# Transformer stack on one core: the feed-forward norm's bias moves ahead of a copy on ScalarE

## The chip, the cores and the metric

The kernel runs on one NeuronCore of a Trainium2 chip, in one launch. The metric is the device time of the whole program in microseconds (us), lower is better. The engines are named as in the profile: PE is TensorE (PEld its weight loads), ACT is ScalarE, DVE is VectorE, POOL is GpSimd, SP issues DMAs. Each engine takes its instructions strictly in the order in which they are written, and waits on semaphores.

## The reference, cut to what matters

The input is `x` of shape (2, 1024, 128) in float32. Four residual blocks follow each other, each behind a layer norm: a causal attention with 16 heads, a stack of six layers, a gated recurrent attention, and the same stack again. The change is in the stack. One of its layers computes:

```python
def ffn_layer(x, g, bln, W1, b1, W2, b2):
    mu = x.mean(-1, keepdims=True)
    var = ((x - mu) ** 2).mean(-1, keepdims=True)
    xn = (x - mu) / jnp.sqrt(var + 1e-05) * g + bln
    hg = xn @ W1 + b1
    a, gate = jnp.split(hg, 2, -1)
    return a * jax.nn.gelu(gate, approximate=False) @ W2 + b2
for i in range(DEPTH):                                   # DEPTH = 6
    x = attn_layer(shift_tokens(x), Wqkv[i], q_scale[i], k_scale[i], Wo[i]) + x
    x = ffn_layer(shift_tokens(x), ln_g[i], ln_b[i], W1[i], b1[i], W2[i], b2[i]) + x
```

`attn_layer` is attention over a local window with 16 heads of 64: it projects q, k and v, normalises q and k, rotates them, takes a softmax over a band of keys, multiplies by v and projects back. The term `+ bln` is the one that moves.

## The kernel before, in words

Activations are kept transposed, 128 features on the partitions and 2048 tokens along the free axis, in four chunks of 512 tokens. A stack is one block of instructions for each engine, a software pipeline over *slots*. A slot takes up a new unit of attention work (a pair of heads on one chunk, 32 units in a layer) and works on older units in their later stages: in the code `a` is the unit begun in this slot, `b` the one begun two slots earlier, `d` four slots earlier. A layer has 32 slots; the layers run in a loop (`pipelined`), with the first and the last partly written out. No scheduler decides the order: each engine does what its function `slot(j, unit)` writes, top to bottom, and semaphores tie the engines together.

The feed-forward part of the same or the previous layer is threaded into these slots. A chunk needs six *steps*, 0 to 5, in six successive slots: mean (0), variance (1), three tiles of hidden features (2, 3, 4: for each, one product for `a` and one for the gate), and the gelu (5). `step` is the step that the slot begins, `before` the one of the slot before. Two chunks are done in each half layer. Step 2 always falls in a slot with odd `j`, as step 4 does, and in odd slots ScalarE also has the inverse norms of q and k (three instructions, lines 1080 to 1085). The last two chunks of each stack are done after the loop by other code, so step 2 occurs 2 stacks x (24 - 2) = 44 times.

What stands around the change in a step-2 slot, by engine:

- DVE multiplies the centred values by the gain and the inverse deviation (line 1268, semaphore `f_norm`).
- ACT does the inverse norms, copies the attention output `oT` out of PSUM (line 1119, `o_cp`), copies the projected values `va` out of PSUM bank 0 (line 1125, `va_cp`), adds the norm's bias in place on `fin` (line 1132, `f_in`; `fin` shows as tile `cen` in the profile), and then takes the eight exponentials of the softmax (line 1138, `exp_done`).
- PE projects the values (line 982, `va_mm`), multiplies `oT` by `wo` (line 996, after `o_cp`), makes the first hidden products from `fin` (line 1003 after `f_in`, line 1018), and opens the next slot with the q product into bank 0 (line 930, after `va_cp`), then lines 939 and 942.
- In the next slot DVE makes the split (line 1235), the copy of the first hidden tile (line 1243) and the product of line 1257; ACT copies the gate (line 1092), which line 949 on PE waits for; POOL adds the halves of the rotation (line 841) once SP's swapping DMAs have landed.

In a chunk that is the first of its layer, line 1003 also waits for the feed-forward weights (`ffw_ld`).

Of the kernel before, what the change touches and what calls it, by code (L numbers as in the profile page):

```python
# [9 lines left out]
ACT = mybir.ActivationFunctionType  # L10
# [40 lines left out]
ONE = 1  # L51
# [575 lines left out]
def stack(rep, ln_call, S, nc, w, c, bank, wide, xT, y, ident, identb, jmean, ln_eps, ss_eps, ss_back,  # L627
# [3 lines left out]
    with ExitStack() as st:  # L631
        def sb(name, shape, dt=F32):
            return st.enter_context(nc.sbuf_tensor(f"b{rep}_{name}", shape, dt))
# [11 lines left out]
        lng = sb("lng", [P, 2])  # L645
# [21 lines left out]
        fin, gel = cen[:, 0, :], cen[:, 1:1 + FT, :]  # L667
# [14 lines left out]
        def twos(u):  # L682
            return PER // 2 * (L0 + u[0]) + u[1] // 2
# [16 lines left out]
        def ffn(u):  # L700
            if u is None or ending(u) or u[1] % HALF >= 2 * FSTEPS:
                return None, None, None
            which, step = divmod(u[1] % HALF, FSTEPS)
            k = 2 * (u[1] // HALF) + which
            return step, k, NC * (L0 + u[0]) + k
# [22 lines left out]
        with nc.Block() as block:  # L728
# [334 lines left out]
            def _(act):  # L1063
# [3 lines left out]
                def slot(j, unit, act=act):  # L1067
                    a, b, d, f, f0 = unit(0), unit(2), unit(4), unit(FLAG), unit(FLAG + 1)
                    step, fk, C = ffn(f)
# [7 lines left out]
                    def inverse_norms(n):  # L1077
                        act.wait_ge(S["ss_mm"], ONE + n + 1)
                        act.wait_ge(S["split_done"], ONE + n)
                        act.activation(rn[:, :], bank[2][:, :], ACT.Ln, bias=ss_eps[:, 0:1], scale=SS_SCALE)\  # L1080
                            .then_inc(S["ln_done"], 1)
                        act.wait_ge(S["ln_done"], ONE + n + 1)
                        act.activation(rhi[:, :], rn[:, :], ACT.Exp, bias=ss_back[:, 0:1], scale=-0.5).then_inc(S["hi_done"], 1)
                        act.wait_ge(S["hi_done"], ONE + n + 1)
                        act.activation(rn[:, :], rn[:, :], ACT.Exp, bias=ss_back[:, 0:1], scale=-0.5).then_inc(S["rn_done"], 1)
# [31 lines left out]
                    if d:  # L1117
                        act.wait_ge(S["pv_mm"], ONE + 2 * UD + 2)
                        act.activation(oT[:, kd % 2, :], bank[7], ACT.Copy).then_inc(S["o_cp"], 1)  # L1119
                    if before == 5:  # L1120
                        act.preload_act_table_set("natural_log_exp_and_others")
                    if a:
# [4 lines left out]
                            .then_inc(S["va_cp"], 1)  # L1127
                    if a and j % 2 and before == 5:
                        inverse_norms(twos(a))
                    if step == 2:  # L1130
                        act.wait_ge(S["f_norm"], ONE + C + 1)
                        act.activation(fin, fin, ACT.Identity, bias=lng[:, 1:2]).then_inc(S["f_in"], 1)
                    if b:
                        UB, kb = um(b)
                        act.wait_ge(S["smax_done"], ONE + UB + 1)
# [5 lines left out]
                    if step == 5:  # L1141
                        act.preload_act_table_set("gelu_and_others")
                        act.wait_ge(S["f_gcp"], ONE + FT * C + FT)
                        act.activation(gel, gel, ACT.Gelu).then_inc(S["f_gelu"], 1)
                pipelined(act, PER, DEPTH, LAG, slot)

                def last_shift(n, act=act):
# [967 lines left out]
```

## Time and profile before

| what | value |
|---|---|
| time, median of 3 runs | 4369.92 us (4368.14 to 4377.39) |
| the profiled execution | 4373.69 us, its span 4372.0 us |
| PE busy | 4078.6 us, 93% |
| DVE busy | 3362.0 us, 77% |
| ACT busy | 3109.2 us, 71% |
| POOL busy | 1797.4 us, 41% |
| mean share of the 16 DMA engines that one queue (q1) takes | 36.7% |

Busy time is summed over the whole span, which the two stacks make up for the most part. Matmuls are pipelined and their ends are modelled, so where PE loses time it shows best as the distance between the starts of two instructions, compared with the same two elsewhere.

### The profile page before, as it was taken

To read this page: it belongs to the slowest core of one execution; us is meant where nothing else is said; L and a number is where in the kernel's file an instruction comes from. 1 tells how busy PE (TensorE), PEld (TensorE's weight loads), DVE (VectorE), ACT (ScalarE), POOL (GpSimd) and SP (SyncE) were. 2 spreads that over 40 slices of the span, in tenths; PEclk is the share of its full clock that TensorE was granted. 3 is DMA by queue.
4 is the path that set the end of the run, shared out by engine and by line. 5 is a ranking of instruction groups with operands and counts; after the bars stand their busy time and mean duration, and the time that the engine had idled before them with its cause. 6 is when DMAs were issued, how large, how long until landed. Compare 5 with 4: busy or idle time off the path is not lost. (4 is left out here: it accounts for less than half of the span.)

```text
span 4372.0 us, 111762 instructions
## 1 busy us (share of the span) xinstructions
PE 4078.6 (93%) x43089; PEld 2415.8 (55%) x43089; DVE 3362.0 (77%) x4981; ACT 3109.2 (71%) x7032; POOL 1797.4 (41%) x1071
## 2 busy tenths in 40 slices
PE   7997999999999999999967589999999999999998
PEld 3443555555555555555536545555555555555554
DVE  5774888888888888888735478888888888888885
ACT  3555777777777777777762267777777777777776
POOL 3112444444444444444404534444444444444442
PEclk7997999999999999999986599999999999999999
DMA  2212444444443444444300044444444444444342
GB/s 43 31 21 72 96 110 101 106 95 103 104 104 93 112 103 96 106 98 104 80 10 3 3 111 107 103 94 106 108 96 109 99 105 96 103 103 107 93 100 49
DMA packets 232516, 380.70 MB, mean 87 GB/s; under 512 B 59365, under 2 KB 122337, under 8 KB 231689
## 3 DMA queue, kind: packets, MB, share of 16 engines
q1 hardware_dynamic: 231560, 372.20, 36.7%
q8 instruction: 370, 6.06, 0.6%
q10 hardware_dynamic: 384, 0.79, 0.1%
q14 instruction: 202, 1.65, 0.1%
HBM read 39.22 MB, written 1.05 MB: 9 GB/s over the span
## 5 line engine op out<-in xcount | busy, mean ns | idle before, releaser
L835 POOL TENSOR_TENSOR b_prob<-b_prob,b_rinv 128x768 f32<-128x768 f32 x384 | 564.2, 1469 | 1797.0 <-DVE b_rinv L1276 1797.0
L841 POOL TENSOR_TENSOR b_prc<-b_prc,b_sws 128x1024 f32<-128x1024 f32 x384 | 906.7, 2361 | 70.8 <-DMA b_sws<-b_prs 70.6
L1138 ACT ACTIVATE b_prob<-ps,b_nmx 128x96 f32<-128x96 f32 x3072 | 748.9, 362 | 0.0
L1211 DVE SCALAR_TENSOR_TENSOR b_prc<-ps,b_qks,b_rot 128x512 f32<-128x512 f32 x768 | 570.6, 743 | 11.8 <-ACT b_sq L1099 11.5
L1213 DVE SCALAR_TENSOR_TENSOR b_prs<-ps,b_qks,b_rot 128x512 f32<-128x512 f32 x768 | 569.5, 742 | 0.0
L1257 DVE TENSOR_TENSOR b_prc<-b_prc,ps 128x512 f32<-128x512 f32 x384 | 263.5, 686 | 384.9 <-PE ps L942 305.4
L1074 ACT ACTIVATE b_pT<-ps 128x512 f32<-128x512 f32 x724 | 434.8, 601 | 129.8 <-PE ps L879 127.9
L879 PEld LDWEIGHTS ps<-ident,b_prob 128*128 128x128 f32 x3072 | 381.5, 141 | 219.8 <-ACT b_pT L1074 121.3
L879 PE MATMUL ps<-ident,b_prob 128*128 128x128 f32 x3072 | 461.4, 273 | 5.9 <-ACT b_pT L1074 5.8
L982 PE MATMUL ps<-b_wqkv,b_xs 128*128 128x256 f32 x1536 | 434.1, 405 | 2.2 <-DVE b_prs L1213 2.2
L1119 ACT ACTIVATE b_oT<-ps 128x512 f32<-128x512 f32 x384 | 226.8, 591 | 293.7 <-PE ps L899 293.7
L930 PE MATMUL ps<-b_xs,b_wqkv 128*128 128x512 f32 x768 | 405.9, 610 | 24.8 <-issue 11.3
L996 PE MATMUL ps<-b_oT,b_wo 128*128 128x512 f32 x768 | 411.8, 618 | 5.6 <-ACT b_oT L1119 5.6
L899 PE MATMUL ps<-b_pT,b_vs 128*64 128x64 f32 x6144 | 399.5, 229 | 0.3
L949 PE MATMUL ps<-b_xs,b_wqkv 128*128 128x512 f32 x768 | 395.6, 597 | 0.0
L899 PE MATMUL ps<-b_pT,b_va 128*64 128x64 f32 x6144 | 380.7, 222 | 0.0
L1231 DVE TENSOR_TENSOR y<-ps,y 128x512 f32<-128x512 f32 x384 | 265.0, 690 | 145.6 <-PE ps L996 145.0
L968 PEld LDWEIGHTS ps<-b_kr,b_prc 64*64 64x64 f32 x12288 | 269.6, 132 | 180.0 <-issue 180.0
L1273 DVE TENSOR_REDUCE b_ssm<-b_prob 128x8 f32<-128x768 f32 x384 | 361.7, 942 | 0.0
L1281 DVE TENSOR_REDUCE b_nmx<-ps 128x8 f32<-128x768 f32 x384 | 351.6, 916 | 7.9 <-PE ps L968 1.4
L968 PE MATMUL ps<-b_kr,b_prc 64*64 64x96 f32 x12288 | 342.1, 249 | 0.0
L899 PEld LDWEIGHTS ps<-b_pT,b_vs 128*64 128x64 f32 x6144 | 309.5, 137 | 46.6 <-ACT b_pT L1074 0.8
(293 smaller groups left out, 7294.5 us busy)
## 6 DMA issues: line engine op xcount, KB each, us to landing
b_sws<-b_prs SPq DMA_DIRECT2D x1536, 128.0 KB
b_vs<-b_va SPq DMA_DIRECT2D x384, 256.0 KB, 3.8
b_wqkv<-in_L_ffn_Wqkv SPq DMA_DIRECT2D x96, 192.0 KB, 3.5
b_xs<-y SPq DMA_DIRECT2D x126, 128.0 KB, 2.3
b_wo<-in_L_ffn_Wo SPq DMA_DIRECT2D x96, 64.0 KB, 3.2
b_xs<-y SPq DMA_DIRECT2D x42, 127.8 KB, 2.3
b_rot<-in_rot SPq DMA_DIRECT2D x2, 2048.0 KB, 7.9
b_w<-in_L_ffn_W SPq DMA_DIRECT2D x24, 170.5 KB
```

Source lines behind the costliest of these rows:

```text
L835: pool.tensor_tensor(prob[:, r, :, P - KEYS:P], prob[:, r, :, P - KEYS:P], rinv[:, r % 2, :].rearrange("p (b a) -> p b a", a=1).broadcast_ ...
L841: pool.tensor_tensor(prc[:, r, :, :], prc[:, r, :, :], sws[:, r % 2, :, :], ALU.add)\
L879: t = pe.transpose(bank[6][:, i * P:(i + 1) * P], prob[:, kd, 4 * e + 2 * h + m, :], ident[:, :])
L899: t = pe.matmul(bank[7][es, n * BLK:(n + 1) * BLK], v[:, es], pT[:, h, 2 * e + m, o * BLK:(o + 1) * BLK], start=(n == 0), stop=(n == NB - ...
L930: pe.matmul(bank[0][:, :], W[:, 0, :], X, start=True, stop=True).then_inc(S["q_mm"], 1)
L968: g = pe.matmul(wide[0][o * BLK:(o + 1) * BLK, e * CH + m * KEYS:e * CH + (m + 1) * KEYS], prc[es, kb, 0, n * BLK:(n + 1) * BLK], kr[es, a ...
L982: m = pe.matmul(bank[0][:, 2 * t * P:2 * (t + 1) * P], xs[:, at:at + P], wqkv[:, 2, p0:p0 + 2, :].rearrange("p a f -> p (a f)"), start=(t ...
L996: pe.matmul(bank[3][:, :], wo[:, pair(d), :], oT[:, kd % 2, :], start=True, stop=True).then_inc(S["wo_mm"], 1)
L1074: act.activation(pT[:, h, :, :], bank[6].rearrange("p (i q) -> p i q", i=4), ACT.Copy)\
L1138: g = act.activation(prob[:, kb, i, P - KEYS:P], wide[0][:, e * CH + m * KEYS:e * CH + (m + 1) * KEYS], ACT.Exp, bias=nmx[:, kb % 2, i:i + 1])
L1211: dve.scalar_tensor_tensor(out=prc[:, r, i, :], in0=bank[i][:, :], scalar=scale, in1=rot[:, 2 * i, t], op0=ALU.mult, op1=ALU.mult)
L1213: dve.scalar_tensor_tensor(out=prs[:, r % 2, i, :], in0=bank[i][:, :], scalar=scale, in1=rot[:, 2 * i + 1, t], op0=ALU.mult, op1=ALU.mult) ...
```

## The change

In the function `slot` of ScalarE the step-2 instruction (wait for `f_norm`, add the bias, raise `f_in`) now stands directly behind the copy of `oT` and ahead of the copy of `va`. Nothing else differs: the same instructions with the same operands, waits and increments.

```diff
@@ -1117,6 +1117,9 @@
                     if d:
                         act.wait_ge(S["pv_mm"], ONE + 2 * UD + 2)
                         act.activation(oT[:, kd % 2, :], bank[7], ACT.Copy).then_inc(S["o_cp"], 1)
+                    if step == 2:
+                        act.wait_ge(S["f_norm"], ONE + C + 1)
+                        act.activation(fin, fin, ACT.Identity, bias=lng[:, 1:2]).then_inc(S["f_in"], 1)
                     if before == 5:
                         act.preload_act_table_set("natural_log_exp_and_others")
                     if a:
@@ -1127,9 +1130,6 @@
                             .then_inc(S["va_cp"], 1)
                     if a and j % 2 and before == 5:
                         inverse_norms(twos(a))
-                    if step == 2:
-                        act.wait_ge(S["f_norm"], ONE + C + 1)
-                        act.activation(fin, fin, ACT.Identity, bias=lng[:, 1:2]).then_inc(S["f_in"], 1)
                     if b:
                         UB, kb = um(b)
                         act.wait_ge(S["smax_done"], ONE + UB + 1)
```

ScalarE's queue in a step-2 slot of the layer loop, before (`b_` is the prefix of the stack's semaphores and tiles, `ps` is PSUM; line 1119 is the copy of `oT`, 1125 that of `va`):

```order
L1085 ACTIVATE b_rn<-b_rn,ss_back 128x512 [waits b_hi_done]
L1119 ACTIVATE b_oT<-ps 128x512 [waits b_pv_mm]
L1125 ACTIVATE b_va<-ps 128x2x2x128 [waits b_va_mm]
L1132 ACTIVATE cen<-cen,b_lng 128x512 [waits b_f_norm]
L1138 ACTIVATE b_prob<-ps,b_nmx 128x96 [waits b_smax_done]
L1138 ACTIVATE b_prob<-ps,b_nmx 128x96 x7
```

The same place in the changed kernel, where the bias is line 1122 and the copy of `va` line 1128:

```order
L1085 ACTIVATE b_rn<-b_rn,ss_back 128x512 [waits b_hi_done]
L1119 ACTIVATE b_oT<-ps 128x512 [waits b_pv_mm]
L1122 ACTIVATE cen<-cen,b_lng 128x512 [waits b_f_norm]
L1128 ACTIVATE b_va<-ps 128x2x2x128 [waits b_va_mm]
L1138 ACTIVATE b_prob<-ps,b_nmx 128x96 [waits b_smax_done]
L1138 ACTIVATE b_prob<-ps,b_nmx 128x96 x7
```

One instruction and its wait have moved up by one place; the queues of all other engines are the same in both. TensorE's queue at that place, in both kernels, from the projection of the values to the q product of the next slot:

```order
L982 MATMUL ps<-b_wqkv,b_xs 128x256 [waits b_pq_done,b_sqq_done]
L982 MATMUL ps<-b_wqkv,b_xs 128x256
L996 MATMUL ps<-b_oT,b_wo 128x512 [waits b_y_add,b_o_cp]
L1003 MATMUL ps<-cen,b_w 128x512 [waits b_f_in]
L1018 MATMUL ps<-cen,b_w 128x512 [waits b_pk_done]
L930 MATMUL ps<-b_xs,b_wqkv 128x512 [waits b_va_cp]
```

Nothing moves here; the two waits whose semaphores the change reorders are those of lines 1003 and 930.

## Rows read from the trace of the kernel before

**Rows 1.** Page, 40 slices: busy tenths of PE, granted clock in tenths.

```profile
PE   7997999999999999999967589999999999999998
PEclk7997999999999999999986599999999999999999
```

**Rows 2.** The bias instruction, line 1132, and who waited for it (us, times).

```profile
L1132 ACT ACTIVATE cen<-cen,b_lng x44: 712/712/714, 581.9 to 4266.5; 128x512 f32<-128x512 f32 x44
  PEld ps L1003: 39.4, 34
  PE ps L1003: 15.5, 44
```

**Rows 3.** Timeline, a step-2 slot: start us, us, engine, line, operation [idle before].

```profile
1024.17 0.74 DVE L1268 SCALAR_TENSOR_TENSOR cen<-cen,b_lng,sqr 128x512 f32<-128x512 f32 x1
...
1026.91 0.58 ACT L1119 ACTIVATE b_oT<-ps 128x512 f32<-128x512 f32 x1
...
1027.54 1.12 PE L996 MATMUL ps<-b_oT,b_wo 128*128 128x512 f32 x2
1027.74 0.60 ACT L1125 ACTIVATE b_va<-ps 128x512 f32<-128x512 f32 x1 [0.25 <-PE ps L982]
1028.23 0.71 ACT L1132 ACTIVATE cen<-cen,b_lng 128x512 f32<-128x512 f32 x1
...
1028.85 1.95 ACT L1138 ACTIVATE b_prob<-ps,b_nmx 128x96 f32<-128x96 f32 x8
1029.00 0.30 PEld L1003 LDWEIGHTS ps<-cen,b_w 128*128 128x128 f32 x2 [1.16 <-ACT cen L1132]
...
1030.82 1.02 PE L930 MATMUL ps<-b_xs,b_wqkv 128*128 128x512 f32 x2
```

**Rows 4.** Timeline, the step-4 slot of the same chunk, to the next slot.

```profile
1047.09 1.13 PE L996 MATMUL ps<-b_oT,b_wo 128*128 128x512 f32 x2
...
1047.63 0.19 PEld L1003 LDWEIGHTS ps<-cen,b_w 128*128 128x128 f32 x1 [0.24 <-issue]
...
1048.06 1.02 PE L1003 MATMUL ps<-cen,b_w 128*128 128x512 f32 x2
...
1049.77 1.02 PE L930 MATMUL ps<-b_xs,b_wqkv 128*128 128x512 f32 x2
...
1056.12 1.02 PE L996 MATMUL ps<-b_oT,b_wo 128*128 128x512 f32 x2
...
1056.58 2.38 POOL L841 TENSOR_TENSOR b_prc<-b_prc,b_sws 128x1024 f32<-128x1024 f32 x1
```

**Rows 5.** Timeline, what follows the step-2 slot of rows 3.

```profile
1029.31 1.11 DVE L1235 SCALAR_TENSOR_TENSOR b_rsp<-b_rhi,b_minus_hi,b_rn 128x512 fp32r<-128x512 f32 x1
...
1030.35 0.74 DVE L1243 TENSOR_SCALAR b_hid<-ps,b_b 128x512 f32<-128x512 f32 x1
...
1031.02 0.69 ACT L1092 ACTIVATE cen<-ps,b_b 128x512 f32<-128x512 f32 x1 [0.23 <-PE ps L1018]
1031.25 0.19 PEld L939 LDWEIGHTS ps<-b_rsp,b_take 128*128 128x128 f32 x1 [0.24 <-issue]
...
1032.42 0.69 DVE L1257 TENSOR_TENSOR b_prc<-b_prc,ps 128x512 f32<-128x512 f32 x1 [1.33 <-PE ps L942]
...
1032.59 1.02 PE L949 MATMUL ps<-b_xs,b_wqkv 128*128 128x512 f32 x2
...
1037.17 1.02 PE L996 MATMUL ps<-b_oT,b_wo 128*128 128x512 f32 x2
```

**Rows 6.** Timeline of PE, first chunk of a layer: first and last of ten places.

```profile
877.83 1.12 PE L996 MATMUL ps<-b_oT,b_wo 128*128 128x512 f32 x2
...
881.20 1.02 PE L930 MATMUL ps<-b_xs,b_wqkv 128*128 128x512 f32 x2
...
4208.18 1.12 PE L996 MATMUL ps<-b_oT,b_wo 128*128 128x512 f32 x2
...
4211.54 1.02 PE L930 MATMUL ps<-b_xs,b_wqkv 128*128 128x512 f32 x2
```

**Rows 7.** Timeline, the q product behind a slot without hidden products.

```profile
1056.97 0.30 PEld L930 LDWEIGHTS ps<-b_xs,b_wqkv 128*128 128x128 f32 x2 [0.66 <-ACT b_va L1125]
```

## Prediction

> **What bounds the kernel now.** I read the page's slices first: in both stacks PE is busy nine tenths or more in every slice, and its granted clock is full there, so a microsecond that PE loses in a slot is a microsecond of the program unless another engine takes it back [rows 1]. The page's chain of waits covers only the last block and says nothing here. Next I asked the one instruction that moves, the bias, who waits for it. It runs 44 times at 0.712 us, and nobody but the hidden product of line 1003 ever waits for it: PE sat idle 15.5 us for it over 44 times, its weight loads 39.4 us over 34 [rows 2]. Those are two views of one wait, not a sum, and the first is too small, since the end of the product ahead is modelled. The size of the wait has to be read from starts.
>
> So I read a step-2 slot in order of time [rows 3]. ACT copies `oT` at 1026.91, sits idle 0.25 us until PE has projected the values, copies `va` at 1027.74, adds the bias at 1028.23 to 1028.94, and PE loads the weights of line 1003 at 1029.00, 0.06 us later. PE had started the `wo` product at 1027.54 and reaches the next slot's q product at 1030.82: 3.28 us from start to start. The step-4 slot of the same chunk has the same instructions on PE in the same order, is also an odd slot, and has no bias to wait for. There the two starts lie at 1047.09 and 1049.77: 2.68 us [rows 4]. The reader is to see that the difference, 0.60 us, is what the bias costs PE, and that it stays: from `wo` product to `wo` product the step-2 slot takes 1037.17 - 1027.54 = 9.63 us [rows 3, 5], the step-4 slot 1056.12 - 1047.09 = 9.03 us [rows 4], again 0.60 apart.
>
> In the first chunk of a layer the distance is 3.37 us, at 877.83 to 881.20 and in all ten such places to 4208.18 to 4211.54 (3.36) [rows 6]; the other 34 places, the first chunks of the two stacks' first layers among them, show about 3.28. The extra 0.09 is the second wait of line 1003, for the weights, which PE takes up only after the first.
>
> **The change, part by part.** Nothing is added or removed, and one instruction goes past one other.
>
> The bias earlier. Its operand is ready: the gain is done at 1024.17 + 0.74 = 1024.91, and ACT begins the copy of `oT` at 1026.91 [rows 3]. ACT starts the next instruction 0.49 us after such a copy (1027.74 to 1028.23), so the bias starts at 1026.91 + 0.49 = 1027.40 and ends at 1028.11; PE can see it at 1028.17, in place of 1029.00. It fills the 0.25 us in which ACT now waits for the projection.
>
> What PE needs. In the step-4 slot the load of line 1003 comes 0.54 us after the `wo` product starts and the product 0.97 us after it [rows 4]. Here these are 1028.08 and 1028.51. The bias is seen 0.09 us after the load is due, but a load takes 0.19 us, so it ends at 1028.36, before the product is due. I take nothing for that: the slot becomes 2.68 us and the gain is 0.60 us. The other end: if the lateness of the load passes on in full, 0.51. In the first chunks the second wait puts the load at 1028.26 to 1028.45, still under the `wo` product, and the gain there is 3.37 - 2.68 = 0.69.
>
> The Trainium skill has a rule on just this point (TensorE: Matmul & The Clock Gate, the step on LDWEIGHTS in what happens when a matmul is issued): weights of the next product are loaded while the present one still streams. If that also holds for a load released late by a semaphore, the lateness costs nothing and the sum is the one I use; if it doesn't, the sum is 44 x 0.51 = 22.4 us. The trace shows loads under a product [rows 4], but none released late in the middle of one.
>
> The copy of `va` later. The bias holds ACT for 1028.85 - 1028.23 = 0.62 us [rows 3], so `va` starts at 1027.40 + 0.62 = 1028.02, not 1027.74, and ends at 1028.62: 0.28 us later than now. Its one waiter on PE is the next q product, whose load is due 0.43 us before the product (the lead that line 1003 has in [rows 4]): even in the shortened slot 1030.82 - 0.60 - 0.43 = 1029.79. There is 1.1 us to spare, since the two hidden products lie between. Cost zero. SP too waits for `va` before it issues the copies of the values, one slot on, later than that.
>
> The exponentials. ACT reaches them at 1028.02 + 0.49 = 1028.51 in place of 1028.85, and all behind them in ACT's queue gains a third of a microsecond. The gate copy of line 1092 now waits 0.23 us for PE [rows 5] and will start about half a microsecond earlier, and the product of line 949 that needs it starts 1032.59 - 1031.71 = 0.88 us after its end [rows 5]; nothing to pay.
>
> Whether the next slot can start 0.60 earlier. DVE does not move at first, because its addition to `y` hangs on the `wo` product, which stays: the split ends at 1029.31 + 1.11 = 1030.42 and is seen at 1030.48. PE's load of line 939 now stands at 1031.25 and will want to be at 1030.65 [rows 5]. It fits with 0.17 us to spare, the tightest place that I find. The copy of the hidden tile ends at 1031.09 or a little after, and DVE now sits idle 1.33 us before line 1257 [rows 5], so it has 0.7 us left. POOL's addition and the swapping DMAs ahead of it keep up with a slot of 9.03 us, with no idle time for a DMA before it [rows 4].
>
> The sum: 34 x 0.60 + 10 x 0.69 = 20.4 + 6.9 = 27.3 us. Bounds: below, 22.4 us if the late load is paid in full. Above, if the three pairs of products ran at the pitch of the two in the step-4 slot, (1049.77 - 1048.06) / 2 = 0.855 each [rows 4], the way from `wo` to q would be 2.57 and the gain 0.71 and 0.80: 34 x 0.71 + 10 x 0.80 = 32.1 us. The value taken is the one that a whole measured slot shows. Against the profiled execution's 4373.69 us it gives 4346.4; that execution was 3.8 us slower than the median of the runs, 4369.92, and from the median it gives 4342.6. I forecast 4343 us.
>
> **The rivals.**
> *The next slot takes part of it back.* The place is line 939, with 0.17 us to spare. If DVE's split gets longer, PE waits for it there. For: the split took 1.11 us behind the step-2 slot [rows 5], longer than the 0.74 of DVE's gain instruction of the same 512 columns [rows 3], so its length depends on what runs beside it. Against: neither its start nor POOL's work beside it moves. If it took half a microsecond more, PE would lose 0.50 - 0.17 = 0.33 of the 0.60, and 44 x 0.27 = 12 us would be left: 4358.
> *Nothing comes of it.* The slot could be set by a loop of DVE, POOL and the swapping DMAs, with PE's wait only showing its slack; 4370. Against: the step-4 slot is 0.60 shorter with the same attention work.
> *Slower: the copy of `va` becomes the wait.* Behind slots without hidden products, PE does wait for `va` before the q product, 0.66 us of idle load time in one case [rows 7]. If that held behind step-2 slots as well, the 0.28 us by which `va` is later would go straight into each: 44 x 0.28 = 12.3 us, 4382. It decides once `va` ends more than 1.1 us later than I work out, which needs the bias to stand waiting for its gain on ACT with `va` and the exponentials queued behind. Against: the gain is ready 2.5 us before.
> *More than forecast*, by the upper bound: 4338.
>
> **How the numbers follow.** A measurement of this kernel can tell about 0.2%, 8.7 us, from no change. Chances: forecast 0.81 (4338 to 4348 by its bounds), more 0.03, part taken back 0.07, nothing 0.06, slower 0.03. Faster by over 0.2% holds in the first three: 0.91; the same 0.06; slower 0.03. The range reaches from just under the upper bound of the gain, 4336, to 4354, where the runs' own scatter of a few us above the median and a part of the second case are in.
>
> **What would show it.** In the changed profile: the copy of `oT`, then the bias 0.49 us later, then `va` without idle time; line 1003's load about 0.6 us after the `wo` product starts, with PE's idle time for the bias gone from 15.5 us to near zero; `wo` to q product 2.68 us in all 44 places; step-2 slots of 9.03 us. It is wrong if PE's loads at line 939 now wait for the split, if line 930's wait for `va` behind step 2, or if the slot stays at 9.63 with the idle time moved elsewhere.

## The result and the profile after

The changed kernel takes 4347.82 us (median of 5 runs, 4342.63 to 4350.86) against 4369.89 us before (5 runs, 4368.14 to 4377.39): ratio 0.9945, 95% interval 0.993 to 0.9959, which is 18 to 31 us faster. A second set, run with the experiments, gave 4348.62 against 4372.28 us, ratio 0.9944 (0.9923 to 0.9965). The profiled execution took 4347.82 us with a span of 4346.1; the one before had 4372.0. The forecast was 4343 us with a range of 4336 to 4354. The medians alone do not say which of the forecast's terms is right: 4348 is also what its lower bound gives, with the late load paid in full (4369.92 - 22.4 = 4347.5). The slots below decide that.

The bias instruction and its waiters in the changed kernel, as in [rows 2]:

```profile
L1122 ACT ACTIVATE cen<-cen,b_lng x44: 708/709/711, 577.7 to 4242.5; 128x512 f32<-128x512 f32 x44
  PEld ps L1003: 10.6, 34
```

The line for matmuls that wait, 15.5 us before, is gone. Weight loads still wait 10.6 us over 34 times, 0.31 us each. That wait lies under a running product, as the timeline of the same slot shows (the columns are those of [rows 3]):

```profile
1018.89 0.74 DVE L1268 SCALAR_TENSOR_TENSOR cen<-cen,b_lng,sqr 128x512 f32<-128x512 f32 x1
...
1021.63 0.58 ACT L1119 ACTIVATE b_oT<-ps 128x512 f32<-128x512 f32 x1
1022.11 0.71 ACT L1122 ACTIVATE cen<-cen,b_lng 128x512 f32<-128x512 f32 x1
...
1022.26 1.12 PE L996 MATMUL ps<-b_oT,b_wo 128*128 128x512 f32 x2
1022.72 0.58 ACT L1128 ACTIVATE b_va<-ps 128x512 f32<-128x512 f32 x1
1022.87 0.19 PEld L1003 LDWEIGHTS ps<-cen,b_w 128*128 128x128 f32 x1 [0.31 <-ACT cen L1122]
1023.20 1.96 ACT L1138 ACTIVATE b_prob<-ps,b_nmx 128x96 f32<-128x96 f32 x8
1023.22 1.02 PE L1003 MATMUL ps<-cen,b_w 128*128 128x512 f32 x2
...
1024.03 1.12 DVE L1235 SCALAR_TENSOR_TENSOR b_rsp<-b_rhi,b_minus_hi,b_rn 128x512 fp32r<-128x512 f32 x1
...
1024.94 1.02 PE L930 MATMUL ps<-b_xs,b_wqkv 128*128 128x512 f32 x2
...
1025.08 0.74 DVE L1243 TENSOR_SCALAR b_hid<-ps,b_b 128x512 f32<-128x512 f32 x1
1025.14 0.69 ACT L1092 ACTIVATE cen<-ps,b_b 128x512 f32<-128x512 f32 x1
...
1025.37 0.19 PEld L939 LDWEIGHTS ps<-b_rsp,b_take 128*128 128x128 f32 x1 [0.24 <-DVE b_rsp L1235]
...
1026.54 0.69 DVE L1257 TENSOR_TENSOR b_prc<-b_prc,ps 128x512 f32<-128x512 f32 x1 [0.73 <-PE ps L942]
...
1031.29 1.02 PE L996 MATMUL ps<-b_oT,b_wo 128*128 128x512 f32 x2
```

Read it from the `wo` product at 1022.26. The bias follows the copy of `oT` by 0.48 us, and `va` follows the bias by 0.61 us without idle time. The load of line 1003 comes 0.61 us behind the `wo` product, its product 0.96 us, the q product 2.68 us, and the next `wo` product 9.03 us. In [rows 3, 5] the last two were 3.28 and 9.63. I read the distance from `wo` to q at all 44 places: it is 2.68 us at 40 and 2.65 at the four of the stacks' first layers. The 44 slots together, from `wo` product to `wo` product, took 424.3 us before and take 397.2 now: 27.1 us. From the first to the last `wo` product, the two stacks together took 3513.3 us before, 3486.9 now and 3486.4 in the second set, at a granted clock of 1.00 throughout.

### The profile page after: what moved, and what is told of

Its sections match the earlier page's. It is cut to its first block and busy times, and to the rows that moved or that the text cites. A ratio compares the mean times of both kernels' runs of the same rounds, so it can differ in the third digit from the quotient of the medians.

```text
span 4346.1 us, 111762 instructions
## 1 busy us (share of the span) xinstructions
PE 4064.4 (94%) x43089; PEld 2420.0 (56%) x43089; DVE 3363.2 (77%) x4981; ACT 3107.2 (71%) x7032; POOL 1800.6 (41%) x1071
## 5 line engine op out<-in xcount | busy, mean ns | idle before, releaser
L930 PE MATMUL ps<-b_xs,b_wqkv 128*128 128x512 f32 x768 | 405.9, 610 | 22.9 <-issue 10.6
```

Source lines behind the costliest of these rows:

```text
L930: pe.matmul(bank[0][:, :], W[:, 0, :], X, start=True, stop=True).then_inc(S["q_mm"], 1)
```

## The experiments

The kernels with no bias and with the bias ahead of the copy of `oT`, between or behind the exponentials are the kernel before with this one edit; all others are cut from the changed kernel. Comments in the diffs are for the reader. Medians are compared with runs of the kernel before on the same chip. "wo to q" is the distance between the starts of the `wo` product and the next q product in step-2 slots; I read it at all 44 places of each trace.

**The bias moved in half of the places.**

```diff
-                    if step == 2:
+                    if step == 2 and fk % 2 == 0:     # ahead of the copy of va
...
+                    if step == 2 and fk % 2 == 1:     # behind the copy of va
```

> The bias stands ahead of the copy of va only for the even chunks of a layer (22 of the 44 places, all ten first chunks of 3.37 us among them) and behind it for the odd ones. Theory T1 (PE waits for the bias, each place is worth 0.60 us, 0.69 in the ten): 12 x 0.60 + 10 x 0.69 = 14 us faster than before, and in the trace the wo-to-q distance is 2.68 us at the 22 and 3.28 (3.23 in a stack's first layer) at the other 22. Rival T2 (a slot-wide limit that the change happened to loosen): not in proportion, distances between the two values.

Measured: 4356.07 against 4370.27 us, ratio 0.9966 (0.9953 to 0.998), 14 us faster. wo to q is 2.68 (2.65) us at 22 places and 3.28 (3.23) at the other 22. The bias lines of this kernel, the early one and then the late one, each with its waiters:

```profile
L1122 ACT ACTIVATE cen<-cen,b_lng x22: 709/709/711, 575.4 to 4184.0; 128x512 f32<-128x512 f32 x22
...
  PEld ps L1003: 3.7, 12
```

```profile
L1135 ACT ACTIVATE cen<-cen,b_lng x22: 712/712/713, 633.4 to 4241.9; 128x512 f32<-128x512 f32 x22
...
  PEld ps L1003: 25.5, 22
  PE ps L1003: 7.3, 22
```

Only the late ones stop a matmul. The 44 slots take 410.3 us, 14.0 less than before. The gain is local and goes with the number of places.

**No bias at all.**

```diff
-                        pe.wait_ge(S["f_in"], ONE + C + 1)
+                        pe.wait_ge(S["f_norm"], ONE + C + 1)
...
-                    if step == 2:
-                        act.wait_ge(S["f_norm"], ONE + C + 1)
-                        act.activation(fin, fin, ACT.Identity, bias=lng[:, 1:2]).then_inc(S["f_in"], 1)
```

> Leaves out the addition of the norm's bias in the 44 places altogether (the output changes): line 1003 waits for the gain on DVE directly, and ScalarE has 0.62 us less to do in each step-2 slot. T1: no more than the changed kernel gains, about 27 us locally against before, wo-to-q 2.68 us, since PE no longer waits for the bias there and the wo product still waits for the oT copy. Rival T3 (the gain came from ScalarE reaching its exponentials and the gate copy a third of a microsecond earlier, not from the bias): another 0.62 us of relief per slot should then bring clearly more, some 50 us in all.

This kernel computes something else, since it leaves the bias out; the count of `f_in` that the code behind the loop waits for is lowered to match. Measured: 4336.64 against 4370.27 us, ratio 0.9928 (0.991 to 0.9945). That is 34 us, 24 to 39 by the interval, which holds the 27 of T1 and not the 50 of T3. wo to q is 2.68 us, the 44 slots take 397.0 us, as in the changed kernel. So relief of ScalarE beyond the wait buys nothing in these slots, and the few microseconds more lie outside the stacks, where time scatters from run to run (below). T3 is out.

**The copy of `va` behind the exponentials.**

```diff
-                    if a:                       # copy of va, ahead of the exponentials
+                    if a and step != 2:
...
+                    if a and step == 2:         # the same copy, behind them
```

> As the changed kernel, but in the 44 step-2 slots the copy of va goes behind the eight exponentials. By my times va would then end about 30.5 on the clock of the step-2 slot of the trace before, and the q load is due at 29.79: 0.7 to 0.8 late on the load, 0.35 to 0.5 on the product that follows it plus a restart of 0.1. T1 with 1.1 us to spare for va: the step-2 slot loses 0.4 to 0.6 us against the changed kernel, 18 to 26 us, and comes out near before (4365 to 4372). T3 (ScalarE's exponentials are what counts, these come 0.5 us earlier here): faster than the changed kernel.

Measured: 4364.49 against 4370.27 us, ratio 0.9991 (0.9978 to 1.0005): the gain is nearly gone. The slots take 414.0 us, 16.8 more than in the changed kernel, a little under what I expected, and still 10.3 less than before; the interval of the ratio allows a gain of at most 9.6 us. The timeline:

```profile
1083.53 1.12 PE L996 MATMUL ps<-b_oT,b_wo 128*128 128x512 f32 x2
...
1085.77 0.65 ACT L1144 ACTIVATE b_va<-ps 128x512 f32<-128x512 f32 x1
...
1086.56 1.10 PE L930 MATMUL ps<-b_xs,b_wqkv 128*128 128x512 f32 x2 [0.19 <-ACT b_va L1144]
```

`va` ends at 1086.42, 2.89 us behind the `wo` product, where the q load was due at 2.25 and the q product at 2.68. The q product is 0.35 us late here, 0.26 to 0.36 over the places. The slower rival's mechanism is real: PE stands waiting for `va`. But it needs a much later `va` than the change makes: there `va` ends at 1.04 us.

**The bias later by one and by two tenths.** One or two ScalarE copies of one column (0.09 us each from start to start) stand between the copy of `oT` and the bias.

```diff
                     if step == 2:
+                        act.activation(junk[:, 0:1], ln_eps[:, 0:1], ACT.Copy)
+                        act.activation(junk[:, 1:2], ln_eps[:, 0:1], ACT.Copy)   # in the second kernel only
                         act.wait_ge(S["f_norm"], ONE + C + 1)
```

> As the changed kernel, with one added ScalarE copy of a single column (into an unused tile) between the copy of oT and the bias: the bias comes 0.15 to 0.25 us later. If a load released late hides under the running product until it ends after the product's due time (0.15 us of room by my sum), PE loses 0 to 0.10 us per place, under 5 us in all, wo-to-q 2.68 to 2.78. If the lateness passes on in full, 0.15 to 0.25 us per place, 7 to 11 us, 2.83 to 2.93.

> As the changed kernel, with two added one-column copies between the copy of oT and the bias: the bias 0.3 to 0.5 us later. With a hidden start the loss per place is the delay less about 0.15 us, plus up to 0.10 for a restarted pair: 0.15 to 0.45 us, wo-to-q 2.83 to 3.13. It gives the slope: from one copy to two, PE's loss should grow by just the length of one copy.

Measured: 4345.46 against 4370.27 us with one, ratio 0.9942 (0.9923 to 0.996); with two one run of 4338.78 us. The kernel with two:

```profile
1076.74 0.19 ACT L1122 ACTIVATE b_junk<-ln_eps 128x1 f32<-128x1 f32 x1
1076.83 0.19 ACT L1123 ACTIVATE b_junk<-ln_eps 128x1 f32<-128x1 f32 x1
...
1076.89 1.12 PE L997 MATMUL ps<-b_oT,b_wo 128*128 128x512 f32 x2
1076.92 0.71 ACT L1125 ACTIVATE cen<-cen,b_lng 128x512 f32<-128x512 f32 x1
...
1077.69 0.36 PEld L1004 LDWEIGHTS ps<-cen,b_w 128*128 128x128 f32 x2 [0.50 <-ACT cen L1125]
1077.86 1.02 PE L1004 MATMUL ps<-cen,b_w 128*128 128x512 f32 x2
```

The load comes 0.61 us behind the `wo` product in the changed kernel, 0.70 with one copy and 0.80 with two; the product comes 0.96, 0.96 and 0.97 us behind it, and wo to q stays 2.68 (2.70 in the ten first chunks with two). I had expected 0.15 to 0.25 us of delay from each copy and, with two, a loss of 0.15 to 0.45 us; the copies are shorter and the loss did not come. At 34 places 0.19 us of additional lateness on the load costs nothing. In the ten first chunks, where line 1003 has its second wait, the load of the kernel with two copies comes later still:

```profile
1166.76 1.13 PE L997 MATMUL ps<-b_oT,b_wo 128*128 128x512 f32 x2
...
1167.64 0.30 PEld L1004 LDWEIGHTS ps<-cen,b_w 128*128 128x128 f32 x2 [0.58 <-issue]
...
1169.46 1.02 PE L931 MATMUL ps<-b_xs,b_wqkv 128*128 128x512 f32 x2
```

It starts 0.88 us behind the `wo` product. The hidden product still starts on time, at 0.96 us, but the q product is 0.02 us late. That is the first loss seen: the room reaches to a load at 0.80 us at least and is used up by 0.88.

**The bias between and behind the exponentials** (both cut from the kernel before).

```diff
                         for i in range(NB):
                             e, m = divmod(i, 4)
+                            if i == 4 and step == 2:    # between; the other kernel: behind the loop
+                                act.wait_ge(S["f_norm"], ONE + C + 1)
+                                act.activation(fin, fin, ACT.Identity, bias=lng[:, 1:2]).then_inc(S["f_in"], 1)
```

> The bias between the fourth and the fifth of the eight exponentials, some 0.35 us later than before (va copy and four exponentials of 0.23 ahead of it, in place of the va copy alone: 0.95 us later). With the bias behind all eight, PE stood idle over 2 us and its granted clock fell to half behind it, and a place cost 3.5 us instead of 1.95. If the delay alone counts while the clock stays full: 0.95 us per place, step-2 slots about 10.6 us, 42 us slower than before (4410 to 4418), granted clock 1.0 behind the wait. If half clock follows here too: 1.8 us or more per place, 80 us slower.

Measured for the one between: 4409.97 against 4372.28 us, ratio 1.009 (1.0071 to 1.0109), 38 us slower. wo to q is 4.21 us, 0.93 more than before, and the slot 10.56, also 0.93 more. The bias ends 2.33 us behind the `wo` product in place of 1.40, so the delay passes on as it is. The matmul that waits:

```profile
1086.87 1.12 PE L1003 MATMUL ps<-cen,b_w 128*128 128x512 f32 x2 [1.26 <-ACT cen L1137]
```

> The other way round: the bias goes behind the eight exponentials, 1.85 to 1.95 us later than in the kernel before. T1: line 1003 waits that much longer in 44 places, wo-to-q about 5.2 us, 80 to 88 us slower than before (4450 to 4458), unless the exponentials being 0.62 us earlier gives some back. T3: no slower, or faster, than before, since the exponentials come earlier.

Measured for the one behind: 4509.21 against 4374.46 us, ratio 1.0306 (1.0287 to 1.0325), 135 us slower. My 80 to 88 was too little. The timeline, then the stretches before, just behind and further behind the wait (us, busy time of PE, PEld, DVE, ACT and POOL with their instructions, granted clock, DMA share, GB/s):

```profile
1115.99 1.12 PE L996 MATMUL ps<-b_oT,b_wo 128*128 128x512 f32 x2
...
1118.47 0.78 ACT L1140 ACTIVATE cen<-cen,b_lng 128x512 f32<-128x512 f32 x1
...
1119.30 1.29 PE L1003 MATMUL ps<-cen,b_w 128*128 128x512 f32 x2 [2.19 <-ACT cen L1140]
...
1120.39 1.92 PE L1018 MATMUL ps<-cen,b_w 128*128 128x512 f32 x2
...
1122.09 1.75 PE L930 MATMUL ps<-b_xs,b_wqkv 128*128 128x512 f32 x2
...
1129.17 1.02 PE L996 MATMUL ps<-b_oT,b_wo 128*128 128x512 f32 x2
```

```profile
1115.90:1119.20 3.30, 1.22 (x4) 0.30 (x2) 2.43 (x4) 3.05 (x11) 2.42 (x2) 1.00 0.00 0
1119.30:1122.90 3.60, 3.60 (x5) 1.50 (x6) 0.75 (x1) 0.56 (x1) 0.00 (x0) 0.62 0.81 183
1123.90:1127.00 3.10, 3.10 (x46) 2.13 (x44) 2.58 (x5) 2.37 (x4) 0.00 (x0) 1.00 0.22 66
```

The bias ends 1.86 us later than in [rows 3], counted from the `wo` product (3.26 in place of 1.40). PE stands idle for 2.19 us, and behind that its granted clock is 0.62 on the mean: for a stretch the lower of its two levels, 1.2 GHz. The pair of line 1018 takes 1.70 us to the q product where it takes 0.86 at full clock. This place costs 3.55 us (13.18 against 9.63), nearly twice the delay. I read the clock of the 3.6 us behind the wait at all 44 places. At 30 of them it was 0.53 to 0.68 and the slot took 13.04 to 13.27 us; at the other 14 it stayed at 1.00 and the slot took 11.48 to 11.57 us, 1.85 more than before, which is the delay and nothing else. The length of the wait does not tell the two kinds apart: the clock fell at 28 of the 34 places with 2.17 to 2.19 us of idle time, and at only 2 of the ten first chunks, which have 2.28. What does, stays open. In all, the 44 slots take 556.6 us, 132 more than before. The error of my forecast is the clock. With an idle time of 1.24 to 1.35 us, in the kernel with the bias between, there is no such second kind: all 44 slots take 10.51 to 10.64 us at a clock of 1.00.

**The bias ahead of the copy of `oT`.**

```diff
+                    if step == 2:
+                        act.wait_ge(S["f_norm"], ONE + C + 1)
+                        act.activation(fin, fin, ACT.Identity, bias=lng[:, 1:2]).then_inc(S["f_in"], 1)
                     if d:
                         act.wait_ge(S["pv_mm"], ONE + 2 * UD + 2)
                         act.activation(oT[:, kd % 2, :], bank[7], ACT.Copy).then_inc(S["o_cp"], 1)
```

> The bias stands ahead of the copy of oT, directly behind the inverse norms. The copy of oT, on which the wo product waits in odd slots, then comes 0.62 us later, and PE waits there in place of at line 1003: the way from the end of the values to the q product grows by 0.6 us and the gain is lost, step-2 slots 9.6 us, time as before (4366 to 4374). If instead the room ahead of the oT copy were free, it would be as fast as the changed kernel or faster.

Measured: 4375.64 against 4374.46 us, ratio 1.0002 (0.999 to 1.0013), as expected. The wait has moved to the `wo` product; the first line is the `wo` product of the slot ahead:

```profile
1083.64 1.02 PE L996 MATMUL ps<-b_oT,b_wo 128*128 128x512 f32 x2
...
1092.60 0.70 ACT L1119 ACTIVATE cen<-cen,b_lng 128x512 f32<-128x512 f32 x1
1093.21 0.57 ACT L1122 ACTIVATE b_oT<-ps 128x512 f32<-128x512 f32 x1
...
1093.83 1.12 PE L996 MATMUL ps<-b_oT,b_wo 128*128 128x512 f32 x2 [0.45 <-ACT b_oT L1122]
```

I had expected step-2 slots of 9.6 us, and that is not where the time went: from the late `wo` product on, the slot takes 9.03 us, as in the changed kernel. It is the stretch ahead of it, from the `wo` product of the slot before, that takes 10.20 us in place of 9.59 (10.19 in the lines above); over the 44 places that is 449.2 against 422.2 us, 27.0 us, which is what the shorter slots give back. Of the five places tried for the bias, one is good: behind `oT`, which PE needs first, and ahead of `va`, which it needs last.

**A better version: the copy of `oT` ahead of the third inverse norm.** In odd slots ScalarE's third inverse-norm instruction (line 1085) still runs when the input of the `oT` copy is there.

```diff
+                    split = a and d and j % 2 and before != 5 and step in (0, 2, 4)
                     if a and j % 2 and before != 5:
-                        inverse_norms(twos(a))
+                        inverse_norms(twos(a), split)      # leaves the third out
...
+                    if split:                              # behind oT and the bias, ahead of va
+                        third_norm(twos(a))
```

> As the changed kernel, and in the odd slots with steps 0, 2 and 4 (110 slots) the copy of oT (and the bias) goes between the second and the third of the three inverse-norm instructions. By the trace before, the copy of oT starts at 1026.91 because the third runs until then, while its input is there at about 1026.70; the wo load then comes 0.2 us earlier, under the running product, and the 0.10 us that a stalled load costs goes: 110 x 0.10 = 11 us faster than the changed kernel at most (4333 to 4340). Rival: the split on DVE or the va copy gets late, nothing gained or some lost.

Measured: 4335.6 against 4374.46 us, ratio 0.9916 (0.9901 to 0.9932), 39 us faster than before, where the changed kernel is 22 and 24 us faster. In this timeline the copy of `oT` is line 1124, the bias 1127, the third norm 1089, the copy of `va` 1135:

```profile
1079.33 0.60 ACT L1124 ACTIVATE b_oT<-ps 128x512 f32<-128x512 f32 x1 [0.44 <-PE ps L899]
...
1079.83 0.71 ACT L1127 ACTIVATE cen<-cen,b_lng 128x512 f32<-128x512 f32 x1
1079.98 0.39 PEld L996 LDWEIGHTS ps<-b_oT,b_wo 128*128 128x128 f32 x2
...
1080.18 1.02 PE L996 MATMUL ps<-b_oT,b_wo 128*128 128x512 f32 x2
1080.44 0.71 ACT L1089 ACTIVATE b_rn<-b_rn,ss_back 128x512 f32<-128x512 f32 x1
...
1081.05 0.59 ACT L1135 ACTIVATE b_va<-ps 128x512 f32<-128x512 f32 x1
...
1082.76 1.02 PE L930 MATMUL ps<-b_xs,b_wqkv 128*128 128x512 f32 x2
```

The load of `wo` is no longer held. A pair of products whose first load comes only as the pair starts (both at 1022.26 in the changed kernel) takes 0.96 us to the next pair; one whose load is 0.17 us or more ahead takes 0.86. So wo to q is 2.58 us. Step-2 and step-4 slots take 8.92 us, 0.11 less than in the changed kernel at most places; over the 88 slots that is 9.5 us. The slots with step 0, which I had counted in, give nothing.

> As e8 (copy of oT between the second and third inverse norm), but in all odd slots that have them, those without feed-forward products too. There the q product waits for the copy of va directly behind the wo product; va comes 0.08 us later than in the changed kernel by my times, the wo product 0.10 earlier: no gain from these slots, so as fast as e8 within 3 us (4332 to 4340). Rival: the freed tenth counts there too, some 8 us faster than e8.

Measured for all odd slots that have these norms: 4333.42 against 4372.28 us, ratio 0.9913 (0.9896 to 0.9931), the same as the version above. The changed kernel, run again on the same chip, took 4348.62 us; the ranges of the runs, 4321.91 to 4345.75 and 4333.63 to 4365.05, overlap. The slots without feed-forward products give no gain that can be told, as expected.

> The changed kernel once more, beside the two others of this call on one chip. T1: each of the 44 places is worth 0.60 or 0.69 us, 27 us in all, and the 22 us between the medians measured first are that plus scatter of stages that the change doesn't touch: a second ratio near 0.994 (0.992 to 0.996), and step-2 slots again 9.03 us. If something outside the slots takes back 5 us each time, the stretches outside would again be longer than before by as much.

Measured beside it, the changed kernel again: 4348.62 us, as given at the top; the 44 slots take 397.1 us, and nothing outside them takes time back regularly: all other slots of the two stacks together took 3089.0 us before, 3089.7 in the changed kernel and 3089.3 in this set. Where the scatter sits can be seen here, since this profiled execution was 10 us longer than the first one of the same kernel. The same stretch ahead of the stack, first in the first execution, then in this one:

```profile
20.00:400.00 380.00, 322.52 (x2086) 148.23 (x2086) 239.29 (x324) 190.78 (x435) 54.44 (x76) 0.90 0.20 36
```

```profile
20.00:400.00 380.00, 332.30 (x2071) 152.71 (x2072) 229.45 (x305) 183.05 (x422) 52.82 (x73) 0.84 0.17 26
```

The granted clock was 0.84 in place of 0.90 there, fewer instructions fit into it, and the first `wo` product of the stack started at 446.7 us and not at 432.0. In the stretch between the stacks, executions with the same slots differ by up to 10 us as well, from the last `wo` product of one stack to the first of the next: 377.8 us in the kernel without the bias, at a mean granted clock of 0.72, and 387.4 in the first execution of the changed kernel, at 0.69.

## Why the prediction was right, point by point

*Line 1003's wait for the bias is a loss of 0.60 us on the bounding engine.* Right, shown from both sides: half the places gave half the gain, 0.93 us more delay cost 0.93 us per slot, the bias one place further up moved the whole 0.61 us to the stretch ahead, and taking the bias out altogether left the slots at 397.0 us. The step-4 slot as the model of a step-2 slot without the wait was exact: 2.68 and 9.03 us in both.

*The bias 0.49 us behind the copy of `oT`, seen 0.09 us late on the load.* Measured 0.48 us, and the load 0.61 us behind `wo` where 0.54 was due. That the lateness would cost nothing was taken without a row for it; the kernels with 0.70 and 0.80 us show it. The reason given, that the load ends before the product is due, is not the limit: at 0.80 us a load of 0.19 us starts only 0.17 us ahead of its product, and the product is on time. The prediction also says that the trace before has no load released late in the middle of a product. It has some, at another pair of products, where the load of line 942 waits for DVE's addition to `y`:

```profile
994.52 0.80 PE L939 MATMUL ps<-b_rsp,b_take 128*128 128x512 f32 x1
...
995.01 0.19 PEld L942 LDWEIGHTS ps<-b_rsp,b_take 128*128 128x128 f32 x1 [0.32 <-DVE y L1231]
995.16 0.40 PE L942 MATMUL ps<-b_rsp,b_take 128*128 128x512 f32 x1
```

The load is 0.15 us ahead of its product where one that waits for nothing is 0.23 ahead, and the product comes 0.64 us behind that of line 939 in either case. At 21 places of that trace the lead is only 0.03 to 0.15 us, and the distance stays 0.63 to 0.64. The bound of 22.4 us could have been argued down from there. The Trainium skill's rule that the next weights load while the present product streams (TensorE: Matmul & The Clock Gate, the step on LDWEIGHTS) holds here for a load that a semaphore releases late: the trace agrees, down to 0.17 us between load and product.

*The second wait in the first chunks goes under the `wo` product.* Right: those slots fell from 9.72 to 9.03 us.

*`va` 0.28 us later costs nothing.* Right. The 1.1 us of room fits the kernel that overspends it: with `va` 1.85 us later still, the q product was 0.26 to 0.36 us late.

*The next slot does not take it back.* Right. Line 939's load came 0.21 to 0.24 us behind the split's end (0.81 to 0.92 before; DVE is now named as its releaser), as the tightest place was to be, without a loss: it is 0.43 us behind the q product in both traces, and the slot behind takes 9.92 us in both. The split's length did not change, 1.12 us against 1.11. The prediction was right that it depends on what runs beside it: in the trace before it takes 0.74 us where POOL's addition overlaps it by less than 0.05 us, and 1.11 where the two overlap by 0.56. DVE's idle time before line 1257 fell from 1.33 to 0.73 us.

*The sum.* 27.3 us forecast, 27.1 read in the slots. Had the late load been paid in full, the slots would have given 22.4. The upper bound's way of 2.57 us from `wo` to q is real too, but it needs the `wo` load not to be held (2.58 us in the better version). The medians differ by 22.1 and 23.7 us, the forecast of 4343 is 5 us off, and both intervals hold 27. The 25.9 us between the profiled spans are 26.4 in the stacks and the rest outside: the stretch ahead of the first is 3.0 us shorter, the one between them 5.7 longer, the tail 2.1 shorter. Single stretches there differ by up to 10 us with TensorE's granted clock. Whether a microsecond or two of the missing ones is more than scatter stays open.

## What to carry to other kernels

When two copies on one engine feed the engine that bounds, put them in the order in which that engine asks for them; what counts is which one it needs first, not which was ready first. Look for a twin of the stalled place that lacks the one wait: the distance between two starts in the twin tells the gain to a few hundredths, where the idle time in the profile (0.35 us here) told about half. Then test the neighbouring places too: one place further up in the queue the same move was worth nothing.

## What the hardware showed that I had not expected

In these runs a short wait on TensorE costs its length, and a longer one can cost nearly twice as much. A delay of the bias by 0.93 us cost 0.93 us in every slot, with an idle time of 1.26 us. A delay of 1.86 us, with 2.19 us idle, cost 1.85 us at 14 places and 3.5 us at the other 30, where the granted clock fell to its lower level (1.2 GHz) for a stretch behind the wait; which places those are does not follow from the length of the wait. And a ScalarE copy of one column, 0.19 us long in the trace, holds the queue for only 0.09 us from start to start.
